# Mask rows of a mixture-of-experts layer: spread by matrix products, or by DMAs from a transposed fp32 mask

## What is computed

```python
x = x + gnn(layernorm(x), adj)     # two hypergraph convolutions, relu and layernorm between
# then, on layernorm(x), a routed feed-forward part:
logits = x @ router_w + router_b                    # 4 experts
topw, topi = top_k(logits, 2); topw = softmax(topw)
mask[t, e] = weight of expert e for node t, or 0    # (512, 4)
h    = silu(einsum('td,edh->teh', x, expert_w) + expert_b)
comb = einsum('te,teh->th', mask, h)
y    = x + comb @ out_w + out_b;  out = x_before + norm_w * y / rms(y)
```

## Time and profile before

| | |
|---|---|
| median of 3 runs | 728.39 us (727.57 to 728.85) |
| the profiled execution's own time | 727.07 us |
| its span, first to last instruction | 725.5 us |
| granted TensorE clock, mean | 0.992 |
| PE busy | 685.5 us (94%) |
| DVE busy | 622.0 us (86%) |
| ACT busy | 530.5 us (73%) |
| POOL busy | 345.2 us (48%) |
| the chain that ended last | PE 87%, DVE 5%, ACT 3%, DMA 1% |

### The profile page before, as it was taken

The page is one execution under the profiler, slowest core; times in us unless marked ns, Lnnn a source line. Parts: engine busy times, 40 slices in busy tenths (PEclk is TensorE's granted clock), DMA queues, the critical chain, the costliest instruction groups (busy, mean ns, idle before and its releaser), DMA issues.

```text
span 725.5 us, 15868 instructions
## 1 busy us (share of the span) xinstructions
PE 685.5 (94%) x5197; PEld 475.7 (66%) x5197; DVE 622.0 (86%) x1542; ACT 530.5 (73%) x1096; POOL 345.2 (48%) x732
## 2 busy tenths in 40 slices
PE   3777999999999999999999999999999999999973
PEld 2464485866758586775858577685857668585663
DVE  3987799898989989898989989898998989898676
ACT  4567868688696868778686877869686786967554
POOL 4142635456373545636354454635455463634444
PEclk9999999999999999999999999999999999999998
DMA  8547449375664938666583946657494756538312
GB/s 285 189 79 241 91 111 246 78 236 117 212 139 134 231 66 247 121 209 137 152 204 61 276 97 226 121 167 180 73 263 98 231 116 195 123 72 190 59 30 59
DMA packets 42590, 111.72 MB, mean 154 GB/s; under 512 B 4160, under 2 KB 5312, under 8 KB 42560
## 3 DMA queue, kind: packets, MB, share of 16 engines
q0 software_dynamic: 13536, 41.42, 32.5%
q1 hardware_dynamic: 29024, 69.92, 27.6%
HBM read 69.91 MB, written 16.25 MB: 119 GB/s over the span
## 4 chain that ended last, share of the span: by engine, by line
PE 87%; DVE 5%; ACT 3%; DMA 1%; issue 1%; POOL 1%; SPq 0%; POOLq 0%; DVEq 0%; ACTq 0%
PE bank L1335 16%; PE bank L1337 16%; PE bank L1336 16%; PE bank L1420 7%; PE bank L1421 7%; PE bank L1446 7%; PE bank L1478 4%; PE bank L1479 4%; PE bank L1389 4%; PE bank L1382 2%; PE bank L1437 2%; DMA b1b<-b 1%; PE bank L1491 1%; PE bank L1370 0%; ACT x L598 0%
## 5 line engine op out<-in xcount | busy, mean ns | idle before, releaser
L1335 PE MATMUL bank<-xth,ewh 128*128 128x512 f16 (+1 forms) x270 | 99.6, 369 | 2.6 <-DVE ewl L840 2.6
L1337 PE MATMUL bank<-xth,ewl 128*128 128x512 f16 (+1 forms) x270 | 99.8, 370 | 0.0
L1336 PE MATMUL bank<-xtl,ewh 128*128 128x512 f16 (+1 forms) x270 | 99.6, 369 | 0.0
L543 ACT ACTIVATE silu<-bank,ebcol,ksc 128x512 f32<-128x512 f32 x120 | 89.6, 768 | 7.7 <-POOL comb L400 3.9
L400 POOL TENSOR_TENSOR comb<-comb,silu 128x1024 f32<-128x1024 f32 x30 | 74.6, 2488 | 0.6 <-DVE silu L917 0.6
L1335 PE MATMUL bank<-w2h,hnth 128*128 128x256 f16 x256 | 70.3, 275 | 0.6 <-issue 0.6
L1336 PE MATMUL bank<-w2l,hnth 128*128 128x256 f16 x256 | 70.4, 275 | 0.0
L1337 PE MATMUL bank<-w2h,hntl 128*128 128x256 f16 x256 | 70.4, 275 | 0.0
L939 DVE SCALAR_TENSOR_TENSOR hntl<-bank,hnth 128x512 f16<-128x512 f32 x64 | 42.7, 687 | 26.6 <-ACT hnth L561 25.2
L1478 PE MATMUL bank<-xsh,h 128*128 128x256 f16 x256 | 59.4, 280 | 2.9 <-DVE xsl L822 2.3
L917 DVE TENSOR_TENSOR silu<-silu,bank 128x1024 f32<-128x1024 f32 x45 | 54.7, 1216 | 8.2 <-ACT silu L543 8.2
(11 more groups left out here) (283 smaller groups left out, 2077.1 us busy)
## 6 DMA issues: line engine op xcount, KB each, us to landing
adjin<-adj SPq DMA_DIRECT2D x16, 1024.0 KB, 5.4
adjtin<-adjt SPq DMA_DIRECT2D x16, 1024.0 KB, 8.2
xin<-x SPq DMA_DIRECT2D x16, 512.0 KB, 7.8
xb<-xn SPq DMA_DIRECT2D x16, 512.0 KB, 4.2
xb<-x POOLq DMA_DIRECT2D x16, 512.0 KB, 8.9
xb<-b POOLq DMA_DIRECT2D x16, 512.0 KB, 5.4
xb<-vadd POOLq DMA_DIRECT2D x16, 512.0 KB, 4.5
out<-x SPq DMA_DIRECT2D x15, 512.0 KB, 4.9
```

The costliest lines, as they stand in the source:

```text
L543: af(silu[:, i % 4, :], bank[E_BANK[i]][:, :], ACT.Silu, bias=ebcol[:, i:i + 1], scale=ksc[:, 2:3]).then_inc(silu_dn, 1)
L1335: mm(outp, lh, rh, start=first, stop=False)
L1336: mm(outp, lh, rl, start=False, stop=False)
L1337: return mm(outp, ll, rh, start=False, stop=last)
```

## The change

The mask is no longer split into fp16 parts for graphs 0 to 14. PE transposes the fp32 mask (four transposes with 4 output partitions), ACT copies the 4x512 fp32 result to `mtf`, and SP issues one DMA for each expert that reads its one row from `mtf` (2 KB on one partition) and writes it to 128 partitions of `mrow` (256 KB). DVE's `combine` reads `mrow` instead of PSUM. `mask_rows` and its waits are gone. The last graph keeps the old way. `mrow` takes the memory of a buffer used at set-up.

```diff
-        absbuf = sb("absbuf", [P, 2, 1024], F32)
+        mrow = sb("mrow", [P, NE, C], F32)
+        absbuf = mrow[:, :, :].rearrange("p (i e) c -> p i (e c)", i=2)
+        mtf = sb("mtf", [NE, C], F32)
@@ SP
+            def spread_mask(f):
+                sp.wait_ge(mf_cp, f + 1)
+                for e in range(NE):
+                    sp.dma_start(mrow[:, e:e + 1, :], mtf[e:e + 1, :].unsqueeze(1).to_broadcast([1, P, C])).then_inc(row_in[e], 16)
             def body(sp, g, odd, conv, ffn, late, prep):
                 if prep:
                     sp.wait_ge(xn_dn, 4 * g + 4)
                     sp.dma_start(xin[:, :, :], x[g + 1]).then_inc(x_in, 16)
+                if late:
+                    spread_mask(g - 2)
+                if prep:
                     sp.wait_ge(h_made, g + 1)
...
             def tail(sp):
+                spread_mask(N - 2)
@@ ACT
             def mask_copy(act, f):
-                act.wait_ge(mt_rdy, f + 1)
-                af(mt16[:, :], bank[MT_BANK][:, 0:256].bitcast(F16), ACT.Copy).then_inc(mt_cp, 1)
+                act.wait_ge(mf_rdy, f + 1)
+                if not (isinstance(f, int) and f == 0):
+                    for e in range(NE):
+                        act.wait_ge(row_in[e], 16 * f)
+                af(mtf[:, :], bank[MT_BANK][0:NE, :], ACT.Copy).then_inc(mf_cp, 1)
@@ DVE
             def combine(f, e):
                 src = silu[:, 2 * (e % 2):2 * (e % 2) + 2, :]
-                m = bank[MB_BANK[e]][:, :].unsqueeze(1).to_broadcast([P, KD, C])
-                dve.wait_ge(mb_rdy, 4 * f + e + 1)
+                m = mrow[:, e, :].unsqueeze(1).to_broadcast([P, KD, C])
+                dve.wait_ge(row_in[e], 16 * f + 16)
...
             def make_mask(f):
...
-                STT(mask[:, :, :], rank[:, :, :], 1.5, wt[:, :, :], ALU.is_lt, ALU.mult).then_inc(r_step, 1)
-                dve.wait_ge(r_step, 9 * f + 8)
-                v.tensor_copy(m16[:, :, 0:NE], mask[:, :, :]).then_inc(r_step, 1)
-                dve.wait_ge(r_step, 9 * f + 9)
-                TT(m16[:, :, NE:2 * NE], mask[:, :, :], m16[:, :, 0:NE], ALU.subtract).then_inc(mask_dn, 1)
+                dve.wait_ge(r_step, 7 * f + 7)
+                STT(mask[:, :, :], rank[:, :, :], 1.5, wt[:, :, :], ALU.is_lt, ALU.mult).then_inc(mf_dn, 1)
@@ PE
             def transposed_mask(f):
-                pe.wait_ge(mask_dn, f + 1)
+                pe.wait_ge(mf_dn, f + 1)
                 for t in range(CT):
-                    ins = nc.tensor.transpose(bank[MT_BANK][:, 0:256].bitcast(F16)[:, P * t:P * t + P],
-                                              m16[:, t, :], ident16[:, :])
-                ins.then_inc(mt_rdy, 1)
-
-            def mask_rows(f, e, g, conv):
...
-                mm(bank[MB_BANK[e]][:, :], sel[:, e, :], mt16[:, :], start=True, stop=True).then_inc(mb_rdy, 1)
+                    ins = nc.tensor.transpose(bank[MT_BANK][0:NE, P * t:P * t + P], mask[:, t, :], ident[:, :])
+                ins.then_inc(mf_rdy, 1)
@@ PE, body
                     expert_half(f, 2)
-                    mask_rows(f, 0, g, conv)
                     expert_half(f, 3)
-                    mask_rows(f, 1, g, conv)
                     expert_half(f, 4)
                     expert_half(f, 5)
-                    mask_rows(f, 2, g, conv)
...
                     expert_half(f, 6)
-                    mask_rows(f, 3, g, conv)
                     expert_half(f, 7)
```

More of the change, by code:

```diff
@@ L187, in build @@
         d_rdy, lg_rdy, mt_rdy = sem("d_rdy"), sem("lg_rdy"), sem("mt_rdy")
-        mb_rdy = sem("mb_rdy")
+        mb_rdy, mf_dn, mf_rdy, mf_cp = sem("mb_rdy"), sem("mf_dn"), sem("mf_rdy"), sem("mf_cp")
+        row_in = [sem(f"row_in{e}") for e in range(NE)]
         e_rdy = sem("e_rdy")
@@ L727, in last_mask @@
             def last_mask(act, h):
-                act.wait_ge(mt_rdy, LAST + h + 1)
+                act.wait_ge(mt_rdy, h + 1)
                 af(mt16[:, T_ROW * h:T_ROW * h + T_ROW], bank[T_R[h]][:, 0:P].bitcast(F16), ACT.Copy).then_inc(mt_cp, 1)
@@ L991, in route @@
                    lg[:, :, :].unsqueeze(3).to_broadcast([P, CT, NE, NE]), ALU.subtract).then_inc(r_step, 1)
-                dve.wait_ge(r_step, 9 * f + 1)
+                dve.wait_ge(r_step, 7 * f + 1)
                 STT(flat(tie[:, :, :, :]), flat(ldf[:, :, :, :]), 0.0, flat(tri[:, :, :, :]), ALU.is_ge, ALU.mult).then_inc(r_step, 1)
-                dve.wait_ge(r_step, 9 * f + 2)
+                dve.wait_ge(r_step, 7 * f + 2)
                 STT(flat(beat[:, :, :, :]), flat(ldf[:, :, :, :]), 0.0, flat(tie[:, :, :, :]), ALU.is_gt, ALU.max).then_inc(r_step, 1)
-                dve.wait_ge(r_step, 9 * f + 3)
+                dve.wait_ge(r_step, 7 * f + 3)
                 v.reduce_sum(rank[:, :, :], beat[:, :, :, :], X).then_inc(r_step, 1)
-                dve.wait_ge(r_step, 9 * f + 4)
+                dve.wait_ge(r_step, 7 * f + 4)
                 STT(lsel[:, :, :], rank[:, :, :], 1.5, lg[:, :, :], ALU.is_lt, ALU.mult).then_inc(r_step, 1)
-                dve.wait_ge(r_step, 9 * f + 5)
+                dve.wait_ge(r_step, 7 * f + 5)
                 v.reduce_sum(lsum[:, :], lsel[:, :, :], X).then_inc(r_step, 1)
-                dve.wait_ge(r_step, 9 * f + 6)
+                dve.wait_ge(r_step, 7 * f + 6)
                 STT(arg[:, :, :], lsum[:, :].unsqueeze(2).to_broadcast([P, CT, NE]), -0.5, lg[:, :, :],
@@ L1010, in make_mask @@
                 TS(wt[:, :, :], th[:, :, :], 0.5, 0.5, ALU.mult, ALU.add).then_inc(r_step, 1)
-                dve.wait_ge(r_step, 9 * f + 7)
-                STT(mask[:, :, :], rank[:, :, :], 1.5, wt[:, :, :], ALU.is_lt, ALU.mult).then_inc(r_step, 1)
-                dve.wait_ge(r_step, 9 * f + 8)
-                v.tensor_copy(m16[:, :, 0:NE], mask[:, :, :]).then_inc(r_step, 1)
-                dve.wait_ge(r_step, 9 * f + 9)
-                TT(m16[:, :, NE:2 * NE], mask[:, :, :], m16[:, :, 0:NE], ALU.subtract).then_inc(mask_dn, 1)
+                dve.wait_ge(r_step, 7 * f + 7)
+                STT(mask[:, :, :], rank[:, :, :], 1.5, wt[:, :, :], ALU.is_lt, ALU.mult).then_inc(mf_dn, 1)
             def finish(q, tiles, last, again):
@@ L1204, in last_route @@
                 s = slice(CG * h, CG * h + CG)
-                step = 9 * LAST + 9 * h
+                step = 7 * LAST + 9 * h
                 dve.wait_ge(lg_rdy, LAST + h + 1)
@@ L1246, in last_weigh @@
                 m = bank[T_MB[h][e // 2]][:, T_ROW * (e % 2):T_ROW * (e % 2) + T_ROW]
-                dve.wait_ge(mb_rdy, 4 * LAST + 4 * h + 2 * (e // 2) + 2)
+                dve.wait_ge(mb_rdy, 4 * h + 2 * (e // 2) + 2)
                 dve.wait_ge(silu_dn, 8 * LAST + 8 * h + 2 * e + 2)
@@ L1625, in last_turn_mask @@
             def last_turn_mask(h):
-                pe.wait_ge(mask_dn, LAST + h + 1)
+                pe.wait_ge(mask_dn, h + 1)
                 for t in range(CG):
@@ L1632, in last_rows @@
             def last_rows(h):
-                pe.wait_ge(mt_cp, LAST + h + 1)
+                pe.wait_ge(mt_cp, h + 1)
                 if h == 0:
```

## The result

The changed kernel takes 1269.06 us (median of 4 runs, 1260.57 to 1271.41), the one before 727.98 us (727.52 to 728.85): ratio 1.743, 95% interval 1.733 to 1.753. The prediction was 1258 us.

What follows compares the result with a forecast made beforehand. PE was taken as the bound (period 41.85 us). Row wait 33.9 us plus clock 1.7 gave 35.6 us a graph, 31.9 for the last, +530 on 727.1: 1257, median 1258; own range 1130 to 1400, full range 740 to 1400.

Steps and rivals of the forecast that it cites:

- How long a row takes: Each mask row's DMA from one SBUF partition: 9.7 us at a sixteenth of the full rate, 38.7 us for four.
- a DMA kept on one engine: Row DMA: its one-partition source might keep it on one engine, giving the same 9.7 us a row.
- What waits behind it: DVE waits for the rows at combine, so hnt_part and PE's v_tile come late: 33.9 us a graph.
- a sign of being wrong: Rows landing within 3 us of one another in the trace after would show the prediction wrong.
- The clock: PE's clock falls to 1.2 GHz after idling: one loss of 1.7 us of full-speed work a graph.
- The queue: Rows stand behind the x load on SP's queue and start at 337.8; without it, 3.7 us earlier.
- PE's gain: Four mask products gone, less slower fp32 transposes: 0.65 us a graph, 9.7 us in all, swallowed by the wait.
- The rival at 718 us: At combine(0): rows land in time, so PE's 9.7 us stand; 718 us; chance 0.07.
- The rival with all paths open: Rows use all DMA paths, 0.6 to 2.2 us each; queue and DVE-POOL lock decide; 750 to 840 us; chance 0.24.
- Its lock: combine with two SBUF operands and POOL's additions hold each other up: up to 3.4 us a graph, 51 us.

Runs made afterwards that it cites:

- the kernels that built it: The changed kernel with each row DMA reading one DRAM row, 838.62 us, or a tile lying on all 128 partitions, 841.93 us.
- the two nearest: Without POOL's two large additions: the kernel before with combine's second operand in SBUF, 734.61 us, and the changed kernel without row DMAs, 733.42 us.

## Why the prediction was right, step by step

- **How long a row takes: right.** 9.7 us were set, 9.6 measured in the graph shown. That one partition gives its data at the pace of a sixteenth of the whole was only a chosen end of a wide range, so part of the hit is luck. The prediction's other reading of the same price, a DMA kept on one engine, falls: the mean share of 16 engines would then be near 0.06, not 0.9. The sources on all partitions, in DRAM and halved now show it; that neighbouring partitions share the path, and that rows lying apart do not share it to the same degree, is shown by the two kernels with two queues.
- **What waits behind it: right.** Mask copy's end to the third W2 tile was 12.47 us; it is now 593.45 - 547.00 = 46.45: 33.98 us more, 33.9 forecast. DVE's idle times, set at 13, 8, 8 and 8, are 13.02, 7.74, 8.08 and 7.30. In four graphs the last two rows are used within some 2 to 3 us of one another, which the prediction had named as a sign of being wrong; the pace of the whole is the same there, since the last `combine` begins 44.7 to 47.6 us after the copy's end.
- **The clock: right in kind, a little small.** 1.7 us a graph were set. The granted clock is at 0.50 in three stretches of the graph. Only the last lies on the path: matmuls of 256 columns step at 0.21 us from 593.45 to about 597.8 instead of 0.11, half of 4.3 us, 2.1 us. 33.98 + 2.1 = 36.1, and this graph's period grew by 36.0. From copy to copy the period is 77.6 us on the mean of the run (74.2 to 81.6), 35.8 us more than the 41.8 before; fifteen times that is 537, and the span grew by 533.5. PE's share fell to 62% and not to 55%, since matmuls at the lower clock are busy longer.
- **The queue: wrong, and hidden by the sum.** The x load ahead was to delay the rows by 3.7 us a graph; moving it saved 0.8, and the last `combine` begins as late in either order (44.1 and 43.7 us after the copy's end). The changed kernel itself has a graph that shows it: the x load is ahead of the rows in 13 graphs, not in 14, as SP issues none before those of graph 13 (at 1091.65), and there the first `combine` begins 15.67 us after the copy's end, as in the graph shown (15.66). It begins clearly earlier in the first and the last graph alone (12.3 and 11.9 us, the last `combine` at 41.8 and 41.6), the one with an x load ahead, the other without. The start at 337.8 plus four clean rows gave the right landing, but not for the reason given; what sets the start is not shown. With two queues, where two rows had nothing ahead, the kernel was no faster either.
- **PE's gain: right that it is swallowed, wrong that it would be worth 9.7 us otherwise.** With neither rows nor additions it was worth at most 1.2 us. The rival at 718 us, which got 0.07, could not have happened even with rows in time: the two SBUF operands alone cost 64 us beside POOL's additions.
- **The rival with all paths open: the mechanism right, the size low.** It had 750 to 840; the kernels that built it took 839 and 842. Its lock was set at up to 51 us and measured 64. (Its row 0 lands at 337.8 + 0.6 = 338.4, not 338.6, which takes 3 us from its 753.) The lock is in the changed kernel too, but costs little there, since in most graphs POOL's additions end long before the next row lands: only in the four graphs with late first rows does the last `combine` take 3.0 to 3.9 us, and the mean of all 45 is 1.43 us instead of 1.23, 9 us in all.

## What to carry to other kernels

A row that must reach all partitions costs, by a DMA from SBUF, all its copies' bytes at the pace of the one place it lies in; price it by a sixteenth of the full rate, and look where neighbouring rows lie. From DRAM the same broadcast was quick (4.0 us from issue to landing in the kernel that goes by way of DRAM). Before an operand is moved from PSUM to SBUF, look which POOL instructions read SBUF at that time: here that step alone cost 9%, more than every product it was to save. Neither the changed kernel nor any of the twelve experiments beats the one before; the two nearest, 1% behind, leave work out.

## What had not been expected of the hardware

- With the path full, issuing itself is slow: the SP queue's instruction for one row DMA took 475 ns at least, 844 ns in the median and 12482 ns at most (60 of them in the changed kernel).
- POOL's `xb<-b`, which needs nothing of the rows, took 18.3 us to land in the median where it had taken 5.4: other DMAs share the 16 engines, which are 0.9 busy with the rows at that time.
- Four rows issued one after another in one queue do not always land evenly: in the kernel with rows first the first came after 29 us and the next two 10 and 3 us later, and four graphs of the changed kernel are like it.
